# Graph attention layer and graph convolution on one core: the product with V moved ahead of the product with W

## What is computed

```python
h = relu(layernorm(x))
s = (h @ Wq.T + bq) @ (h @ Wk.T + bk).T
w = adj * exp(s);  w = w / w.sum(-1)
x1 = x + w @ (h @ Wv.T + bv)
h1 = relu(layernorm(x1))
A = adj + I;  r = A.sum(-1) ** -0.5
out = x1 + (A * r[:, None] * r[None, :]) @ (h1 @ W + b)
```

## Time and profile before

| | us |
|---|---|
| median of 3 runs | 1683.4 |
| profiled execution, its own time | 1685.13 |
| its span, first to last instruction | 1683.3 |
| TensorE busy in the span | 1657.5 (98%) |
| TensorE weight loads, beside it | 1506.2 (89%) |
| VectorE | 1369.1 (81%) |
| ScalarE | 757.2 (45%) |
| GpSimd | 555.8 (33%) |
| chain that ended last, share of TensorE | 97% |
| mean granted TensorE clock | 0.996 of full |

### The profile page before, as it was taken

One profiled execution on the slowest core, in us unless ns is written; L12 is line 12 of the kernel. 1 busy time (PEld: TensorE's weight loads), 2 busy tenths in 40 slices (PEclk: granted clock), 3 DMA queues, 4 the chain that ended last, 5 costly groups with the idle time before them and its releaser, 6 DMA issues.

```text
span 1683.3 us, 33110 instructions
## 1 busy us (share of the span) xinstructions
PE 1657.5 (98%) x10828; PEld 1506.2 (89%) x10828; DVE 1369.1 (81%) x3285; ACT 757.2 (45%) x1546; POOL 555.8 (33%) x586
## 2 busy tenths in 40 slices
PE   7999999999999999999999999999999999999996
PEld 5899999999999999999899899999999999999996
DVE  5888888888888888888888888888888888888874
ACT  3354454444444444444544544544544444444442
POOL 1323333333333333333243243233333333333331
PEclk9999999999999999999999999999999999999998
DMA  5455455455455465464454454554554554554530
GB/s 177 120 117 146 117 126 146 107 136 143 104 143 140 103 145 139 96 154 133 102 152 128 110 147 125 118 146 119 124 146 110 133 144 103 142 139 102 147 93 29
DMA packets 494413, 212.63 MB, mean 126 GB/s; under 512 B 402496, under 2 KB 427072, under 8 KB 494400
## 3 DMA queue, kind: packets, MB, share of 16 engines
q1 hardware_dynamic: 492480, 210.89, 50.0%
q10 hardware_dynamic: 1920, 1.58, 0.3%
HBM read 146.28 MB, written 66.13 MB: 126 GB/s over the span
## 4 chain that ended last, share of the span: by engine, by line
PE 97%; DVE 1%; DMA 1%; ACT 0%; issue 0%; POOL 0%; ACTq 0%; POOLq 0%; DVEq 0%; SPq 0%
PE ps L638 32%; PE ps L639 32%; PE ps L640 32%; PE ps L648 1%; DMA late<-in_L_gnn_Wq_w_dram 0%; DMA x_in<-in_x_dram 0%; DVE w_in L458 0%; DVE w_lo L451 0%; ACT wvt_hi L321 0%; DVE st_x L471 0%; ACT w_hi L323 0%; ACT late L347 0%; ACT h_hi L349 0%; POOL rs_x L298 0%; POOL hat_hi L270 0%
## 5 line engine op out<-in xcount | busy, mean ns | idle before, releaser
L347 ACT ACTIVATE late<-late,nb,sc 128x512 f32<-128x512 f32 x128 | 103.6, 809 | 509.2 <-DVE nb L542 509.2
L270 POOL TENSOR_TENSOR hat_hi<-adjt,eye 128x512 fp32r<-128x512 f32 x64 | 82.6, 1291 | 629.4 <-DVE ht_lo L610 617.3
L638 PE MATMUL ps<-ht_hi,m_hi 128*128 128x256 f32 x1024 | 287.4, 281 | 0.8 <-DVE wvt_lo L448 0.8
L639 PE MATMUL ps<-ht_lo,m_hi 128*128 128x256 f32 x1024 | 288.0, 281 | 0.0
L640 PE MATMUL ps<-ht_hi,m_lo 128*128 128x256 f32 x1024 | 287.5, 281 | 0.0
L291 POOL TENSOR_TENSOR xb<-xb,bv_row 128x512 f32<-128x512 f32 x128 | 164.8, 1309 | 256.0 <-DMA xb<-in_x_dram 256.0
L638 PE MATMUL ps<-w_hi,z_hi 128*128 128x512 f32 x512 | 202.7, 396 | 1.6 <-DVE z_lo L575 1.5
L639 PE MATMUL ps<-w_lo,z_hi 128*128 128x512 f32 x512 | 202.6, 396 | 0.0
L640 PE MATMUL ps<-w_hi,z_lo 128*128 128x512 f32 x512 | 202.3, 395 | 0.0
L638 PE MATMUL ps<-wvt_hi,ht_hi 128*128 128x512 f32 x512 | 202.2, 395 | 0.0
L640 PE MATMUL ps<-wvt_hi,ht_lo 128*128 128x512 f32 x512 | 202.1, 395 | 0.0
(11 more groups left out here) (106 smaller groups left out, 4322.7 us busy)
## 6 DMA issues: line engine op xcount, KB each, us to landing
x_in<-in_x_dram SPq DMA_DIRECT2D x64, 512.0 KB, 6.3
xb<-in_x_dram SPq DMA_DIRECT2D x64, 512.0 KB, 7.2
out_dram<-late SPq DMA_DIRECT2D x128, 256.0 KB, 2.1
h_scratch<-h SPq DMA_DIRECT2D x62, 512.0 KB, 3.8
h_blocks<-h_scratch SPq DMA_DIRECT2D x248, 128.0 KB, 4.8
adj_in<-in_adj_dram SPq DMA_DIRECT2D x64, 256.0 KB, 2.9
adj_blocks<-in_adj_dram SPq DMA_DIRECT2D x256, 64.0 KB, 2.5
dn_row<-dn_scratch SPq DMA_DIRECT2D x64, 128.0 KB, 2.9
```

Source lines behind the costliest of these rows:

```text
L270: pool.tensor_tensor(hat_hi[:], adjt[:], eye[:], ALU.add).then_inc(hat_hi_ready, 1)
L347: act.activation(h1[:, t, :], x1[:, t, :], ACT.Relu, scale=sc_1[:, t:t + 1], bias=nb_1[:, t:t + 1])
L638: pe.matmul(dst, a_hi[:, c, cols], b_hi[:, c, :], start=(c == 0), stop=False)
L639: pe.matmul(dst, a_hi[:, c, cols], b_lo[:, c, :], start=False, stop=False)
```

## The change

TensorE's order in a step becomes G, V, scores, Z, product with V, product with W. The banks of the product with V are (6, 0) instead of (6, 2), so the second half goes where G and the scores were, and G of the next step waits for x1. VectorE makes x1, its statistics and the scale of the second norm at the end of the graph's own step, instead of at the start of the next. In the last two thirds of a step it now does: turning of h, p, p_lo, z_lo, x1b, z_lo, s_sum and sd, a copy of the score bias, x1, statistics with ht_lo in between, ht_lo, y of the first half, the scale, y of the second half. The score bias is computed early, into `vk_next`, and copied to `vk` by a product with ones. GpSimd's hat ops wait for sd instead of the last ht_lo. ScalarE does exp and p_hi ahead of z_hi. SyncE's program is not edited. In the last step d has a tile of its own (`d_last`). The diff, cut to its core, by engine. The banks, and GpSimd's wait:

```diff
-        O = (6, 2)
+        O = (6, 0)
...
                     pool.wait_ge(p_lo_ready[1], this - 1)
-                    if main:
-                        pool.wait_ge(ht_lo_ready[1], this)
+                    pool.wait_ge(sd_ready, this - 1)
```

ScalarE's wait (its z_hi loop of two lines moves from ahead of exp and p_hi to behind them, unchanged):

```diff
-                        act.wait_ge(vk_ready[t], this)
+                        act.wait_ge(vk_next_ready[t], this)
```

VectorE's new functions (the bodies of attention_out, norm_1, scale_1 and layer_out were in `step`):

```diff
+            def keep_bias(this):
+                for t in range(NT):
+                    dve.wait_ge(vk_next_ready[t], this)
+                dve.tensor_tensor(vk[:], vk_next[:], ones[:, 0:NT], ALU.mult).then_inc(vk_ready, 1)
...
+            def attention_out(this):
+                dve.wait_ge(xb_ready, this)
+                for t in range(NT):
+                    dve.wait_ge(o_done[t], this)
+                    dve.reciprocal(rinv[:, t:t + 1], ps[:, O[t], HD:HD + 1]).then_inc(rinv_ready[t], 1)
+                    dve.wait_ge(rinv_ready[t], this)
+                    dve.scalar_tensor_tensor(halves(x1[:, t, :]), ps[:, O[t]:O[t] + 2, 0:HD], rinv[:, t:t + 1],
+                                             halves(xb[:, t, :]), ALU.mult, ALU.add).then_inc(x1_ready[t], 1)
+
+            def norm_1(this, between):
+                for t in range(NT):
+                    dve.wait_ge(x1_ready[t], this)
+                    last = dve.bn_stats(st_1[:, t, :], x1[:, t, :])
+                last.then_inc(bn_1_done, 1)
+                dve.wait_ge(bn_1_done, this)
+                between()
+                for t in range(NT):
+                    last = dve.bn_aggr(mv_1[:, t, :], st_1[:, t, :])
+                last.then_inc(mv_1_done, 1)
+                dve.wait_ge(mv_1_done, this)
+                dve.tensor_scalar(ve_1[:], mv_1[:, :, 1], EPS, None, ALU.add).then_inc(ve_1_done, 1)
+
+            def scale_1(this):
+                dve.wait_ge(dn_ready, this)
+                dve.wait_ge(rs_1_done, this)
+                dve.tensor_tensor(sc_1[:], rs_1[:], dn[:], ALU.mult).then_inc(sc_1_done, 1)
+                dve.wait_ge(sc_1_done, this)
+                dve.scalar_tensor_tensor(nb_1[:], mv_1[:, :, 0], -1.0, sc_1[:], ALU.mult,
+                                         ALU.mult).then_inc(ln_1_ready, 1)
+
+            def layer_out(t, this, scale):
+                if not isinstance(this, int) or this > 1:
+                    dve.wait_ge(stored, (this - 1) * (16 * NT))
+                dve.wait_ge(o1_done[t], this)
+                dve.wait_ge(x1b_ready[t], this)
+                dve.scalar_tensor_tensor(y[:, t, :], ps[:, O1 + t, :], scale[:, t:t + 1], x1b[:, t, :],
+                                         ALU.mult, ALU.add).then_inc(y_ready[t], 1)
```

VectorE's step, its start:

```diff
+                    scale = d if main else d_last
+                    dve.tensor_tensor(scale[:], dn[:], ones[:, 0:NT], ALU.mult).then_inc(d_ready, 1)
                     if main:
                         transpose_adjacency(this, prev)
                         turn_dn(this, prev)
+                        if ahead:
+                            score_bias(this + 1)
+                    else:
+                        for t in range(NT):
+                            layer_out(t, this - 2, d)
                     for t in range(NT):
                         dve.wait_ge(h1_ready[t], this - 1)
```

VectorE's step, from the turning of h on:

```diff
                     transpose_h(this)
+                if main:
+                    dve.wait_ge(adjt_ready, this)
+                    for t in range(NT):
+                        dve.wait_ge(e_ready[t], this)
+                        dve.tensor_tensor(p[:, t, :], e[:, t, :], adjt[:, t, :], ALU.mult).then_inc(p_ready[t], 1)
+                if main:
+                    for t in range(NT):
+                        dve.wait_ge(p_hi_ready[t], this)
+                        dve.tensor_tensor(p_lo[:, t, :], p[:, t, :], p_hi[:, t, :].bitcast(fp32),
+                                          ALU.subtract).then_inc(p_lo_ready[t], 1)
+                if prev:
+                    z_low(0, this - 1)
                     for t in range(NT):
                         dve.scalar_tensor_tensor(x1b[:, t, :], b_row[:], sd[:, t:t + 1], x1[:, t, :],
                                                  ALU.mult, ALU.add).then_inc(x1b_ready[t], 1)
+                    z_low(1, this - 1)
                 if main:
...
                     dve.tensor_tensor(sd[:], s_sum[:], dn[:], ALU.mult).then_inc(sd_ready, 1)
                 if main and ahead:
+                    if not prev:
+                        score_bias(this + 1)
+                    keep_bias(this + 1)
+                if main:
+                    if prev:
+                        dve.wait_ge(h1_ready[1], this - 1)
+                    attention_out(this)
...
+                if main:
+                    norm_1(this, lambda: ht_low(0, this + 1, turned[0]) if ahead else None)
+                if main and ahead:
+                    ht_low(1, this + 1, turned[1])
+                if prev and ahead:
+                    layer_out(0, this - 1, d)
+                if main:
+                    scale_1(this)
+                if prev and ahead:
+                    layer_out(1, this - 1, d)
+                if not main and not ahead:
+                    for t in range(NT):
+                        layer_out(t, this - 1, d_last)
```

TensorE's waits (the loop of the scores moves from behind Z to ahead of it, that of the product with W from ahead of the product with V to behind it, with their waits, unchanged):

```diff
                 if main:
+                    if prev:
+                        pe.wait_ge(x1_ready[1], this - 1)
                     pe.wait_ge(ht_lo_ready[0], this)
                     pe.wait_ge(ht_lo_ready[1], this)
...
-                        if ahead and not prev and t:
-                            pe.wait_ge(ht_lo_ready[0], this + 1)
-                            pe.wait_ge(ht_lo_ready[1], this + 1)
```

More of the change, by code:

```diff
@@ L513, in step @@
                 if prev:
[L515 to L526, removed]
+                    scale = d if main else d_last
+                    if older and main:
                         dve.wait_ge(y_ready[1], this - 2)
                     dve.wait_ge(dn_ready, this - 1)
-                    dve.wait_ge(bn_1_done, this - 1)
@@ L571, in step @@
                     transpose_h(this)
[L572 to L581, removed]
-                                                 ALU.mult, ALU.add).then_inc(x1b_ready[t], 1)
                 if main:
@@ L600, in step @@
                 if main and ahead:
+                    if not prev:
[5 more added lines that the diff above has]
+                    attention_out(this)
+                if ahead and not main:
+                    for j in range(2):
+                        ht_low(j, this + 1, ps[:, HT + j, :])
+                    bias_products()
+                    wv_and_w_low()
@@ L689, in step @@
                                 (ht_hi, ht_lo), cols, (wvt_hi, wvt_lo)).then_inc(v_done[t], 1)
+                if main:
+                    pe.wait_ge(g_lo_ready[1], this)
+                    for t in range(NT):
+                        cols = slice(t * P, (t + 1) * P)
+                        product(ps[:, G + t, 0:N], DC,
+                                (g_hi, g_lo), cols, (ht_hi, ht_lo)).then_inc(s_done[t], 1)
                 if prev:
@@ L699, in step @@
                             last.then_inc(z_done[m // 2], 1)
-                if main:
-                    pe.wait_ge(g_lo_ready[1], this)
-                    for t in range(NT):
-                        cols = slice(t * P, (t + 1) * P)
-                        product(ps[:, G + t, 0:N], DC,
-                                (g_hi, g_lo), cols, (ht_hi, ht_lo)).then_inc(s_done[t], 1)
                 if ahead and not prev:
@@ L720, in step @@
                         bias_and_wv_products()
+                if main:
+                    pe.wait_ge(p_lo_ready[1], this)
+                    if not prev:
+                        pe.wait_ge(consts_ready, 2)
+                    pe.wait_ge(v_lo_ready[1], this)
+                    if prev:
+                        pe.wait_ge(x1_ready[0], this - 1)
+                    for t in range(NT):
+                        cols = slice(t * P, (t + 1) * P)
+                        for a, width in enumerate((HD + 2, HD)):
+                            last = product(ps[:, O[t] + a, 0:width], NT, (p_hi, p_lo), cols,
+                                           (v_hi[:, :, a, 0:width], v_lo[:, :, a, 0:width]))
+                        last.then_inc(o_done[t], 1)
                 if prev:
```

89 lines of the change are left out of this document (27 added, 62 removed).

## The result

| | before | after |
|---|---|---|
| median of four runs (lowest to highest), us | 1683.38 (1682.77 to 1685.77) | 1811.24 (1808.19 to 1816.68) |
| profiled execution, its span, us | 1685.13, 1683.3 | 1814.22, 1812.4 |
| mean step, first matmul of G to that of the next, us | 25.47 | 27.63 |
| mean granted clock of the span | 0.996 | 0.993 |

A forecast was written before the change was run, and what follows sets the result against it. TensorE bounds the kernel before; the change makes a 28.16 us circle through SyncE bind instead, 2.7 over 25.45. 1685.1 + 61 x 2.7 (165) - 1 for the ends = 1849, median 1.7 less: 1848 us, range 1785 to 1885.

The forecast's parts named there:

- The circle: Loop from turning of h through y, SyncE's store and loads to the next turning: 28.16 us against TensorE's 25.45.
- Turning to the second p: VectorE, two turnings of h (1.22 us) and one p (0.34): 1.56 us.
- Second p to Y: VectorE's chain from second p's start to the end of the step's second y: 12.4 us.
- the full wait for hat_lo: VectorE's first ht_lo is held until GpSimd's hat_lo ends, so it finishes 0.7 to 0.8 us later.
- Y to turning: From second y's end through SyncE's queue, xb load and GpSimd's rs_x to the next turning of h: 14.2 us.
- TensorE's waits: Idle time each step: some 1.9 us for p_lo before the product with V, 0.8 for ht_lo before G.
- The ends: Last step's gap shrinks to some 3.7 us (-4.2), start costs +1 to +4; taken together as -1 us.
- The signs: Expected if right: TensorE's two waits, about 28 us steps, turning waiting, SyncE waiting less for y, first ht_lo over 1.3.
- TensorE staying the bound: Rival: xb and h_blocks land early enough that the turning never waits; about 1682 us, chance 4%.
- ht_lo ahead of hat_lo: Rival: the circle binds but VectorE's ht_lo goes first and loses nothing; circle 27.4 us, 1799 us, chance 20%.
- The slower case: Rival: xb lands as in the step shown, or rs_1 is late; circle 28.7 to 29.3, 1880 to 1915 us, 12%.
- What I had called covered: TensorE's waits for g_lo or z_lo were held covered; s_sum's wait for dn_row at worst 0.2 us, taken as 0.

The follow-up runs named there:

- experiment 2: Kernel after the change, with GpSimd's hat_hi, hat and hat_lo moved behind dn: 1762.8 us, 1.0459 of the kernel before.
- experiment 4: Kernel after the change, with one extra 0.66 us VectorE operation (a copy of x1b) between z_lo and s_sum: 1857.48 us, 1.1014 of before.
- experiment 1: Kernel after the change, with SyncE's stores of y one step later, behind the h_blocks loads: 1708.59 us, 1.0145 of before.
- experiment 6: Kernel before the change, with SyncE's stores of y one step later, behind the h_blocks loads: 1683.97 us, 0.9995 of before.
- experiment 7: Kernel after the change, with both the stores of y one step later and GpSimd's hat ops behind dn: 1815.17 us, 1.0776 of before.
- experiment 5: Kernel after the change, with the extra 0.66 us VectorE operation ahead of h1_lo: median 1829.52 us, 1.0877 of before, runs from 1816.0 to 1838.0.
- experiment 9: Kernel after the change, with stores of y one step later and both ht_lo ahead of the row sums: 1680.78 us, 0.998 of before.

## Why the prediction was right, and where it was off

**The circle, by its pieces.** It was to be turning, p, y, store, h store, xb, turning: 28.16 us; it is 27.60. Turning to the second p: 1.56 predicted, 1.54 measured. Second p to Y: 12.4 predicted, 12.41 measured, with the full wait for hat_lo in it; experiment 2 puts that wait at 0.88, where the prediction had 0.8 (12.4 against 11.6), and experiment 4 shows that an operation on this piece is paid whole. Y to turning: 14.2 predicted, 13.64 measured. This is the term that was mis-sized: 0.56 x 61 = 34 of the 37 us. The step behind it was "I take 14.2, nearer the median, because a step takes the later of two transfers". The sum with the median landing was 13.9, and the maximum over two transfers that was to lift it never came: h_blocks had landed 0.86 us before the turning in the mean, and in all passages but the last the turning followed nb_x by the same 0.20, so xb alone set the time. (In the last passage, which makes no rs_x, the turning stood right behind v_lo and waited for no transfer.) The mean landing of xb was 7.05 and not 7.2, and rs_x started 2.51 behind the start of the adds and not 2.64, which makes the other 0.3.

**That the circle binds at all** is shown by experiment 1: with the stores of y moved, 103 us are gone. Experiment 6, the same edit in the kernel before, brings nothing, so the late place is no gain by itself. One argument of the prediction was none: "Before, it had room, because only 10.5 us of VectorE's work lay between a turning and the Y after it". In the step shown 14.98 + 10.47 is 25.45, and the two pieces of any steady step add up to the step, bound or not. The room before is shown by VectorE's wait inside the second piece (p waited 0.38 for e) and by experiment 6.

**TensorE's waits.** Predicted 1.9 us for p_lo and 0.8 for ht_lo a step; in the step shown 1.34 and 0.69. In the mean it was 59.1 / 52 = 1.14 for p_lo and, without the 6.04 of the head, 39.4 / 57 = 0.69 for ht_lo. The prediction's two add up to the whole 2.7 by which it made the step longer; the recorded gaps do not, since a gap costs more than its record (last section).

**The ends.** The tail's gap was to be 3.7 (3.6 measured), the head +1 to +4 (+2.6 measured): together -1, measured -1.2.

**The signs.** Four of the five came as forecast: the two waits of TensorE, the longer step, VectorE's wait for rs_x (86.2 us in 62 steps) and the first ht_lo at 1.62. One came out the other way: SyncE waited more for y and not less, 697.7 us in all against 510.2 before. It had issued the rest of its step by then, and y, now the last thing that VectorE makes in a step, was what it stood for.

**The rivals.** TensorE staying the bound needed 11.5 us from Y to the turning; the shortest steady passage was 12.45 (the last passage, where nothing waited for a transfer and TensorE had no gap, had 11.15), the mean 13.64. ht_lo ahead of hat_lo did not happen (57 of the first halves took over 1.5 us, and none of the steady ones 0.69), though its 1799 lies nearer to the result than my 1848. That is luck: its circle of 27.4 was short by the wait that it left out (0.8), and the transfers in it were long by 0.56. The slower case had the landing of the step shown, 8.3; the mean was 7.05, and the scale waited for rs_1 in only two steps. Its circle was also added up wrongly at the lower end: 15.0 + 1.56 + 12.4 is 28.96, the 0.3 for rs_1 alone gives 28.46, and neither is the 28.7.

**What I had called covered.** g_lo, z_lo and dn_row: no wait in a steady step, as predicted. It was wrong to carry that over to experiment 7, where g_lo became the bound. And the prediction's circle was not the only one near: with it cut, 25.84 remained, since p, the attention output and ht_lo of a step hang together with TensorE's next G. I had not worked that circle out, and to cut it too was worth 28 us (1708.6 to 1680.8).

**What stays open:** half of the spread in experiment 5; whether hat_lo alone makes ht_lo late in experiment 1; and why the piece from Y to the turning varies from 12.45 to 15.15 between steady steps. The runs show only that the same load of xb lands sooner where the stores of y are not just ahead of it (median 5.3 in experiment 1 against 6.9 after, 3.7 in experiment 6 against 7.2 before).

## What to carry to other kernels

When an operation is moved to a later place on one engine, follow its result through the in-order queue of the issuing engine: a store that waits at the end of a step holds up every load behind it, and the work between the last load and that store becomes a circle whose length is to be compared with the bound engine's step. Cut the circle at the cheapest edge (here, issue the store a step later), then look for the next circle, since a repair that is free while another circle binds may have its own price. And when a step takes the later of two transfers, check which one leads before adding anything for the other. Whether a circle has room is not seen from its length, which equals the step in every steady trace, but from the waits inside it.

## What the runs showed of the hardware that was not expected

**Half clock after short gaps.** In the kernel after, TensorE's granted clock fell to half four times in steady steps, for 3.4 us each (from 323.8, 989.4, 1320.5 and 1596.9), each time 0.4 to 1.1 us after the end of a gap of 1.9 to 2.4 us ahead of the product with V. A longer gap of 2.46 and three of 1.96 to 2.21 elsewhere left the clock alone. The window view, a gap and what followed, for one of either kind:

```profile
321.46:323.38 1.92, 0.00 (x1) 0.00 (x0) 1.72 (x5) 1.26 (x4) 0.00 (x0) 1.00 0.75 113
323.76:327.17 3.41, 3.41 (x19) 3.41 (x18) 3.38 (x11) 1.20 (x4) 0.00 (x0) 0.50 0.18 29
...
735.74:738.20 2.46, 0.00 (x1) 0.00 (x0) 2.26 (x6) 1.26 (x4) 0.00 (x0) 1.00 0.52 102
738.20:741.60 3.40, 3.40 (x26) 3.35 (x27) 3.39 (x8) 1.50 (x3) 0.00 (x0) 1.00 0.23 36
```

The kernel before has no gap over 0.1 us in its steady steps and no such stretch there; experiments 1 and 7, with gaps of at most 1.5 us in steady steps, have none either. The length of the gap alone does not tell which it will be.

**A gap costs more than it shows.** In experiment 1 a recorded gap of 0.17 us made the step 0.37 longer; in the step shown of the kernel after, gaps of 2.03 stand for 2.52 (27.97 against 25.45), two of them. So each costs 0.2 to 0.25 beyond its record. In a stream the matmuls of 256 columns start 0.12 apart and are recorded with 0.28, so the last one before a gap is recorded 0.16 past the time at which its successor would have started. The first one behind a gap takes 0.36 to 0.39, and its successor starts 0.19 to 0.23 behind it.

**Tiny operations wait too.** ve_x, 128x2, takes 0.65 us where it falls under the adds of xb (815.46) and ends with the first of them (814.78 + 1.28); the same operation on the other statistics takes 0.17. In experiment 9 the copy of the score bias, 128x2 too, takes 1.19 instead of 0.16.
